# Input load on a second queue, the first norm ahead of the range chain, and one-hot operands widened by ScalarE

## The reference, cut to what matters

```
xn  = (x - mean(x)) / sqrt(var(x) + 1e-5)          # per node
hp  = xn @ W                                        # 625 x 512 by 512 x 512
agg = segment_sum(hp[src] * edge_w[:, None], dst)   # 20000 edges into 625 nodes
x   = x + relu(agg) + linear_attention(xn)          # and then everything else
```

## Time and profile before

| | us |
|---|---|
| median of 3 runs (lowest, highest) | 1215.78 (1212.98, 1218.05) |
| the profiled execution, its own time | 1213.48 |
| its span in the trace | 1211.9 |
| TensorE busy | 1091.0 (90%) |
| VectorE busy | 553.2 (46%) |
| ScalarE busy | 362.5 (30%) |
| GpSimd busy | 118.4 (10%) |
| window loop, first matmul | 42.49 after the span's start |

### The profile page before, as it was taken

One profiled execution on the slowest core, in us unless ns is written; L12 is line 12 of the kernel. 1 busy time (PEld: TensorE's weight loads), 2 busy tenths in 40 slices (PEclk: granted clock), 3 DMA queues, 4 the chain that ended last, 5 costly groups with the idle time before them and its releaser, 6 DMA issues.

```text
span 1211.9 us, 20096 instructions
## 1 busy us (share of the span) xinstructions
PE 1091.0 (90%) x7246; PEld 732.4 (60%) x7247; DVE 553.2 (46%) x1370; ACT 362.5 (30%) x919; POOL 118.4 (10%) x183
## 2 busy tenths in 40 slices
PE   4788999999998749999997399999999999987898
PEld 2577746467775515555553277787577778554653
DVE  7888748644544501111111335453405545865340
ACT  1012212045554301122222145553135455022330
POOL 1013360020000420111110230000000000000000
PEclk9999999999999669999999699999999999998899
DMA  4000384000000679400999350000111000000001
GB/s 125 35 1 2 100 211 200 0 27 27 28 1 1 244 249 396 185 17 17 371 412 389 92 233 27 28 27 6 65 53 44 27 10 2 35 1 0 1 9 34
DMA packets 19105, 113.09 MB, mean 93 GB/s; under 512 B 4906, under 2 KB 6433, under 8 KB 14948
## 3 DMA queue, kind: packets, MB, share of 16 engines
q1 hardware_dynamic: 13406, 100.95, 22.1%
q0 software_dynamic: 5632, 11.23, 3.5%
HBM read 103.04 MB, written 9.11 MB: 93 GB/s over the span
## 4 chain that ended last, share of the span: by engine, by line
PE 78%; DVE 10%; DMA 5%; issue 3%; ACT 2%; DVEq 1%; POOL 1%; SPq 0%; POOLq 0%; ACTq 0%
PE psum L768 9%; PE psum L588 8%; PE psum L936 8%; PE psum L917 7%; PE psum L791 6%; PE psum L822 5%; PE psum L773 5%; PE psum L804 5%; PE psum L655 4%; PE psum L1021 3%; PE psum L1043 3%; PE psum L606 3%; DMA arena<-in_moe_b 3%; PE psum L949 2%; PE psum L727 2%
## 5 line engine op out<-in xcount | busy, mean ns | idle before, releaser
L588 PE MATMUL psum<-arena 128*125 128x512 f32 x320 | 142.2, 600 | 0.0
L1138 ACT ACTIVATE arena<-arena,small 125x625 f32<-125x625 f32 x120 | 97.0, 809 | 89.9 <-DVE small L1499 89.9
L768 PE MATMUL psum<-arena 128*128 128x313 f32 (+1 forms) x384 | 110.6, 438 | 2.0 <-ACT arena L1077 0.7
L917 PE MATMUL psum<-arena 128*64 128x512 f32 x448 | 100.3, 601 | 6.4 <-DMA arena<-in_moeW 4.9
L1203 ACT ACTIVATE arena<-psum,cols 128x64 f32<-128x64 f32 x224 | 47.5, 361 | 194.4 <-PE psum L923 194.4
L588 PEld LDWEIGHTS psum<-arena 128*125 128x125 f32 x320 | 60.2, 191 | 72.7 <-issue 71.2
L936 PE MATMUL psum<-arena 128*64 128x256 f32 x896 | 99.8, 381 | 3.6 <-DMA arena<-in_moe_b 1.9
L768 PEld LDWEIGHTS psum<-arena 128*128 128x128 f32 x384 | 71.2, 192 | 30.7 <-issue 2.2
L1499 DVE CUSTOM_DVE_ANT_0 arena<-psum,cnt_adj 125x625 f32<-125x625 f32 x80 | 61.5, 806 | 59.1 <-PE psum L791 59.1
L1146 ACT ACTIVATE arena<-psum 125x500 f32<-125x500 f32 x120 | 63.8, 584 | 81.9 <-PE psum L804 81.9
L936 PEld LDWEIGHTS psum<-arena 128*64 128x64 f32 x896 | 63.4, 137 | 36.1 <-ACT arena L1203 5.2
(11 more groups left out here) (266 smaller groups left out, 1402.7 us busy)
## 6 DMA issues: line engine op xcount, KB each, us to landing
arena<-in_moeW SPq DMA_DIRECT2D x16, 4096.0 KB, 17.9
arena<-in_att SPq DMA_DIRECT2D x36, 256.0 KB, 2.8
arena<-in_l1W SPq DMA_DIRECT2D x2, 2048.0 KB, 15.9
token_rows<-arena POOLq DMA_DIRECT2D x19, 128.0 KB, 5.1
rows<-in_rows SPq DMA_DIRECT2D x1, 2240.0 KB
expert_rows<-arena POOLq DMA_DIRECT2D x17, 128.0 KB, 4.9
arena<-token_rows POOLq DMA_DIRECT2D x16, 128.0 KB, 7.8
arena<-in_gnnWo SPq DMA_DIRECT2D x2, 1024.0 KB, 6.2
```

What stands on the lines that cost most here:

```text
L588: mm = pe.matmul(bank(b, NP, D), srcT[:, k, c * NP:(c + 1) * NP], w[:, k, :], start=(k == 0), stop=(k == KC - 1))
L768: mm = pe.matmul(bank(b, P, width), aw[:, w, k, :], srcT[:, k, o:o + width], start=(k == 0), stop=(k == KC - 1))
L917: mm = pe.matmul(psum[q * TT:(q + 1) * TT, 512 * b:512 * b + D], xsT[:, k4, :], EW1[par][:, k4, o:o + D], start=(k4 == 0), stop=(k4 == KC ...
L1138: act.activation(Sx[u % 3][h], Sx[u % 3][h], ACT.Exp, bias=small[0:NP, 80 + n:81 + n], scale=-1.0, accum_out=small[0:NP, 120 + n:121 + n]) ...
```

## The change

Three things are done. The two loads of x are issued by ScalarE at its start and no longer by SP behind the edge loads; ScalarE also runs one dummy square root, which brings its table load forward. VectorE applies the first norm ahead of the range chain, and TensorE makes the sum over windows behind the first `hp` chunk and the bounds row behind the second, in banks 2 and 3. And the operands with an innermost step of 0 are written out by ScalarE (`widened`) into `hot_dst` itself, in two halves of 82 and 83 tiles, so that VectorE compares and multiplies in place, on rows of 32 packed 16-bit values; four passes of 5280 elements become eight of 2624 or 2656.

```
@@ block.sync
-            for p in SPLIT:
-                sp.dma_start(xres[p], ins["x"][p]).then_inc(ld_x, 16)
             sp.wait_ge(ld_x, 32)
@@ block.tensor
-            pe.wait_ge(range_cols, 1)
-            pe.matmul(bank(5, NW, WMIN), upper[0:NW, 0:NW], w_loops, start=True, stop=True).then_inc(range_cum, 1)
             rows_to_cols("xnT0", N1, lambda c: pe.wait_ge(ln_out, c + 1))
             stage_out(pe, "xnT0")
+            ring_ready(0)
+            product_chunk("hp", T1, ring[0], 0)
+            pe.wait_ge(range_cols, 1)
+            pe.matmul(bank(2, NW, WMIN), upper[0:NW, 0:NW], w_loops, start=True, stop=True).then_inc(range_cum, 1)
+            product_chunk("hp", T1, ring[0], 1)
             pe.wait_ge(range_cols, 2)
-            pe.matmul(bank(4, 1, WMIN), w_cols[:, 2:3], ident[0:NW, 0:WMIN],
+            pe.matmul(bank(3, 1, WMIN), w_cols[:, 2:3], ident[0:NW, 0:WMIN],
                       start=True, stop=True).then_inc(range_rows, 1)
-            product_rows("hp", T1, 0)
+            for c in range(2, NC):
+                product_chunk("hp", T1, ring[0], c)
...
-            pe.wait_ge(dst_one, 1)
-            pe.wait_ge(dst_parts, 3)
+            pe.wait_ge(dst_one, 2)
+            pe.wait_ge(dst_parts, 6)
@@ block.scalar
+            for p in SPLIT:
+                act.dma_start(xres[p], ins["x"][p]).then_inc(ld_x, 16)
+            act.wait_ge(consts, 2)
+            act.activation(small[0:1, 94:95], onesf[0:1, 0:1], ACT.Sqrt)
+
+            def widened(dst, src, t, ready):
+                n = t.stop - t.start
+                act.activation(dst[:, t, :], src[:, t].unsqueeze(2).to_broadcast([NP, n, DW]), ACT.Copy).then_inc(ready, 1)
+
+            act.wait_ge(edge_low, 1)
+            for t in tile_halves:
+                widened(hot_dst4[:, :, 3, :], low, t, wide_low)
+            act.wait_ge(edge_parts, 3)
+            widened(hot_dst4[:, :, 0, :], w_part[:, 0, :], tile_halves[0], wide_parts)
             deviation(0)
+            widened(hot_dst4[:, :, 0, :], w_part[:, 0, :], tile_halves[1], wide_parts)
             cols_out("xnT0", T1)
+            for v in (1, 2):
+                for t in tile_halves:
+                    widened(hot_dst4[:, :, v, :], w_part[:, v, :], t, wide_parts)
             rows_out("hp", N2)
@@ block.vector
             norm_moments()
+            norm_apply(0, xres, N1)
             ve.wait_ge(range_turned, 1)
...
-            norm_apply(0, xres, N1)
             ve.wait_ge(range_cum, 1)
...
-            ve.tensor_tensor(hot_dst4[:, :, 3, :], low.unsqueeze(2).to_broadcast([NP, TP, DW]),
-                             iota_dst.unsqueeze(1).to_broadcast([NP, TP, DW]), ALU.is_equal).then_inc(dst_one, 1)
             ve.wait_ge(range_rows, 1)
-            ve.tensor_copy(bounds, bank(4, 1, WMIN)).then_inc(range_ready, 1)
-            ve.wait_ge(dst_one, 1)
+            ve.tensor_copy(bounds, bank(3, 1, WMIN)).then_inc(range_ready, 1)
+            for h, t in enumerate(tile_halves):
+                ve.wait_ge(wide_low, h + 1)
+                ve.tensor_tensor(hot_dst4[:, t, 3, :], hot_dst4[:, t, 3, :],
+                                 iota_dst.unsqueeze(1).to_broadcast([NP, t.stop - t.start, DW]),
+                                 ALU.is_equal).then_inc(dst_one, 1)
+            ve.wait_ge(dst_one, 2)
             for v in range(3):
-                ve.tensor_tensor(hot_dst4[:, :, v, :], hot_dst4[:, :, 3, :],
-                                 w_part[:, v, :].unsqueeze(2).to_broadcast([NP, TP, DW]), ALU.mult).then_inc(dst_parts, 1)
+                for h, t in enumerate(tile_halves):
+                    ve.wait_ge(wide_parts, 2 * v + h + 1)
+                    ve.tensor_tensor(hot_dst4[:, t, v, :], hot_dst4[:, t, v, :], hot_dst4[:, t, 3, :],
+                                     ALU.mult).then_inc(dst_parts, 1)
```

More of the change, by code:

```diff
@@ L175, in build @@
         hot_dst = arena[0:NP, o_D:o_D + TP * 2 * DW].bitcast(BF16)
+        tile_halves = [slice(0, TP // 2), slice(TP // 2, TP)]
         hot_dst4 = hot_dst.rearrange("p (t v d) -> p t v d", v=4, d=DW)
@@ L289, in build @@
         dst_one, dst_parts = sem("dst_one"), sem("dst_parts")
+        edge_low, edge_parts, wide_low, wide_parts = (
+            sem("edge_low"), sem("edge_parts"), sem("wide_low"), sem("wide_parts"))
         hot_ready, hot_free = sem("hot_ready"), sem("hot_free")
@@ L1334, in _ @@
             ve.wait_ge(win_ready, 1)
-            ve.tensor_copy(low[:, 0:ET], low_i)
-            ve.tensor_copy(w_part[:, 0, 0:ET], w_hi)
+            ve.tensor_copy(low[:, 0:ET], low_i).then_inc(edge_low, 1)
+            ve.tensor_copy(w_part[:, 0, 0:ET], w_hi).then_inc(edge_parts, 1)
             ve.scalar_tensor_tensor(key[:, 0:ET], win, 1024.0, srcf, ALU.mult, ALU.add)
@@ L1339, in _ @@
             link(ve.tensor_scalar(w_mid.bitcast(I32), w_rest.bitcast(I32), -65536, None, ALU.bitwise_and))
-            ve.tensor_copy(w_part[:, 1, 0:ET], w_mid)
-            ve.tensor_tensor(w_part[:, 2, 0:ET], w_rest, w_mid, ALU.subtract)
+            ve.tensor_copy(w_part[:, 1, 0:ET], w_mid).then_inc(edge_parts, 1)
+            ve.tensor_tensor(w_part[:, 2, 0:ET], w_rest, w_mid, ALU.subtract).then_inc(edge_parts, 1)
             ve.wait_ge(consts, 16)
@@ L1369, in _ @@
             ve.tensor_copy(w_loops, n_i[:, 1:2].to_broadcast([NW, WMIN])).then_inc(range_cols, 1)
-            ve.scalar_tensor_tensor(w_cols[:, 1:2], w_cols[:, 0:1], 64.0, n_i[:, 1:2], ALU.mult,
-                                    ALU.add)
-            norm_apply(0, xres, N1)
+            link(ve.scalar_tensor_tensor(w_cols[:, 1:2], w_cols[:, 0:1], 64.0, n_i[:, 1:2], ALU.mult,
+                                         ALU.add))
             ve.wait_ge(range_cum, 1)
-            ve.scalar_tensor_tensor(w_cols[:, 2:3], bank(5, NW, 1), 16384.0, w_cols[:, 1:2], ALU.mult,
+            ve.scalar_tensor_tensor(w_cols[:, 2:3], bank(2, NW, 1), 16384.0, w_cols[:, 1:2], ALU.mult,
                                     ALU.add).then_inc(range_cols, 1)
-            ve.tensor_tensor(hot_dst4[:, :, 3, :], low.unsqueeze(2).to_broadcast([NP, TP, DW]),
-                             iota_dst.unsqueeze(1).to_broadcast([NP, TP, DW]), ALU.is_equal).then_inc(dst_one, 1)
             ve.wait_ge(range_rows, 1)
-            ve.tensor_copy(bounds, bank(4, 1, WMIN)).then_inc(range_ready, 1)
-            ve.wait_ge(dst_one, 1)
+            ve.tensor_copy(bounds, bank(3, 1, WMIN)).then_inc(range_ready, 1)
[5 more added lines that the diff above has]
+            ve.wait_ge(dst_one, 2)
             for v in range(3):
-                ve.tensor_tensor(hot_dst4[:, :, v, :], hot_dst4[:, :, 3, :],
-                                 w_part[:, v, :].unsqueeze(2).to_broadcast([NP, TP, DW]), ALU.mult).then_inc(dst_parts, 1)
+                for h, t in enumerate(tile_halves):
+                    ve.wait_ge(wide_parts, 2 * v + h + 1)
+                    ve.tensor_tensor(hot_dst4[:, t, v, :], hot_dst4[:, t, v, :], hot_dst4[:, t, 3, :],
+                                     ALU.mult).then_inc(dst_parts, 1)
             ve.wait_ge(range_ready, 1)
```

## The result

| | before | after |
|---|---|---|
| median of 20 runs (lowest, highest), us | 1215.67 (1212.02, 1218.83) | 1218.93 (1213.52, 1222.55) |
| span of the profiled execution, us | 1211.9 | 1219.8 |
| window loop, first matmul, us after the start | 42.49 | 47.18 |

The ratio is 1.0025, 95% interval 1.0014 to 1.0037: slower by 3 us, within the half per cent that counts as no change here. The time forecast was 1217.3, and the measured 1218.93 lies in the range given, 1211.5 to 1221.5.

A forecast was written before the change was run, and what follows sets the result against it. The start-up was taken as bound by VectorE, about 1 us ahead of TensorE, and by the edges' landing; reordering -2.1 and later edges +3.7 gave +1.6 us, 1215.1 profiled, 1217.3 as median with 2.30 added; range 1211.5 to 1221.5.

The forecast's parts named there:

- (b): Rival: VectorE's in-place passes do not run packed and stay at 5.64 us each; +10.9 and +1.6, 1228.2 us; chance 0.07.
- D: Moment the edge loads land and VectorE starts: 6.06 us before, forecast 9.8, later by 3.7, bounds 0 and 4.9 later.
- equal bytes: Edge loads and x share DMA engines with equal bytes from both queues; edges done at 8.1 us, landing at 8.8.
- x first: Upper bound for the edge loads: they land last on their DMA engines, behind x, at 11.0 us.
- From D to the loop: Start-up from the edges' landing to the window loop: D + 34.3 instead of D + 36.4, a gain of 2.1 us.
- VectorE's two waits ahead of `bounds`: VectorE was to stand idle for nearly 8 us while TensorE makes the sum and the row behind two `hp` chunks.
- The widening, not the statistics, set the root: On ScalarE, three widenings of 2.42 us end at D + 8.6, the variance at D + 8.0; root done at D + 8.8.
- Rival (a): The edge loads keep their time, D below 8.2, at best 6.06; -2.1 us at best, median 1213.7; chance 0.25.
- break-even at D = 8.2: Landing time of the edge loads at which the change neither gains nor loses: 8.2 us after the start.
- shortening VectorE's passes alone: Before the window loop VectorE leads TensorE's own way by about 1 us only, so this alone buys 1 us.
- Rival (c): VectorE's sequencer does not run six instructions ahead, so its register load ends at D + 37.8; +3.6 us, 1220.9; chance 0.10.
- The loop behind: The window loop, once started, takes the same time as before; otherwise the prediction is wrong altogether.

The follow-up runs named there:

- `a_again`: The changed kernel without an edit, run once more; median 1219.06 us, ratio 1.0037 to the kernel before.
- `a_x_on_sp`: The changed kernel with SP issuing x again, behind the three edge loads; median 1214.02 us, ratio 0.9991 to the kernel before.
- `h_widening_only`: The kernel before with ScalarE's widenings, the dummy root and the packed passes only; median 1214.59 us, ratio 0.9984 to the kernel before.
- `c_sum_first`: The changed kernel with x back on SP behind the edges, and TensorE's sum over windows ahead of the first `hp` chunk; 1211.76 us, ratio 0.9979 to before.
- `i_x_behind_table`: The changed kernel with x still issued by ScalarE, but only behind its table load and dummy root; 1215.72 us, ratio 0.9987 to the kernel before.

## Why the prediction was right, and where it was not

The forecast, slower by some 1.6 us and not measurably changed, held in sign and class. The class alone proves little, as all the rivals but (b) lay mostly within it, and the rise was about half of the 3.3 us between the two medians. Point by point:

- **D.** The term that was mis-sized. I took 9.8, between equal bytes (8.8) and x first (11.0). It was 11.25, 11.12 and 11.05 in three executions with x issued at 1.04, thus the upper bound. The model of equal bytes was wrong: from 4 us on the packet counts show about one edge row for one row of x, and a row of x is 16 times as large, so that only 105 of 375 edge rows are through at 8 us, and 121 of the 125 rows of x. That is 1.3 to 1.5 us more than was summed. The Trainium skill, DMA: Bandwidth & Descriptors, section Queues, rings and completion order, has the engines take turns packet by packet; had I priced it with one row of x for one edge row, as the counts from 4 us on have it, about 8 of the 75 edge rows of an engine would have passed beside its 8 rows of x, and D would have come out near the upper bound. The page's packets of some 9 to 17 descriptors are not what these counts show.
- **From D to the loop.** D + 34.3 was summed; `a_again` has 45.24 - 11.12 = 34.1. The parts: the root ends 8.4 behind D (summed 8.8), three widenings 6.97 (7.26), `hp` starts at D + 14.4 (14.7), halves 1.46 (1.45). VectorE's two waits ahead of `bounds`, summed as nearly 8 us, are 4.77 and 3.61 in `a_again`. The widening, not the statistics, set the root, as summed: it began at 19.46, when the third widening was through, 0.3 behind the variance. In `a_x_on_sp`, with x late, the statistics did.
- **The profiled run of after** starts its loop 1.9 later than `a_again`, at D + 35.9: the chunk at half rate, which the sum did not have.
- **Rival (a) and its 1213.7.** The edges did not keep their time, so (a) is out. Its sum was wrong besides: D + 34.3 took x as landed, and with D near 6 it is not, though the rows had x at 11.02 and the statistics ready for it at D + 4.19. `a_x_on_sp` has D at 6.17, a wait of 1.41, and the loop at D + 35.4: 0.9 us under the kernel before, 1.7 when both are counted from the landing of x, and not 2.1. By time it is 0.9991 (0.9972 to 1.0009), which shows no gain for certain. The break-even at D = 8.2 is untouched by this: there the statistics would start at 12.4, when x had landed in every run with that issue. Right was that shortening VectorE's passes alone buys little: `h_widening_only` buys 0.3 by the loop, 0.9984 by time.
- **Rival (b)**, unpacked passes, is out: 1.46 a half, 2.83 without the widening. Section 5.1 of the Vector Engine (DVE) Microarchitecture Reference of the Trainium skill gives such operands two elements a cycle, and the trace agrees: 11.7 us against 11.0, the estimate from its 0.96 GHz without a fixed cost.
- **Rival (c)** is out. The register load on VectorE's sequencer starts at 38.3, behind the compare, with six multiplies still ahead of it in the engine:

```profile
L342 DVEq TENSOR_LOAD <-arena x1: 1608/1608/1608, 38.3 to 38.3; - x1
```

- **The loop behind.** I had said that it would have to take the same time. From the loop's start to the end of the span it takes 1169.4 us before, 1172.6 after and 1172.7 in `a_again`, but from 1167.4 (`c_sum_first`) to 1175.6 (`i_x_behind_table`) in kernels that differ nowhere in it. The span of one execution therefore says little of a change of 3 us; the start of the loop and the medians say it.

## What to carry to other kernels

A load that is moved to another queue to start sooner also starts ahead of what the first queue has still to issue. Look which load the first consumer waits for, how large its rows are beside the mover's, and keep the large rows behind the small ones in time, on whichever queue. And when a long pass is shortened, ask by how much it led: here 10 us taken off VectorE's passes bought under 1 by the start of the loop (`h_widening_only`), and more came only with an earlier start of TensorE's work (`c_sum_first`, 2.4 by the loop, 0.9979 by time). Whether an earlier x adds to that the times do not tell.

## What the runs showed of the hardware that was not expected

**Small rows behind large ones.** Edge rows of 640 B, issued in the same 1.1 us as rows of 10 KB on a second queue, let VectorE start at 11.05 to 11.25 instead of 6.06; with x issued at 2.56, and its first rows moving before 4 us, it started at 5.62. Why the last hundred edge rows pass x there, and not in the first case, no run shows: turns of one row each would have held them up as well. It stays open.

**A chunk at half rate, and a granted clock of 1.00 that is not a record.** In the changed kernel's profile the weight loads of the first `hp` chunk come 0.85 us apart, then 0.43:

```profile
27.48 0.33 PEld L589 LDWEIGHTS psum<-arena 128*125 128x125 f32 x1 [0.52 <-issue]
...
30.09 0.19 PEld L589 LDWEIGHTS psum<-arena 128*125 128x125 f32 x1 [0.24 <-issue]
```

The granted clock of that stretch (third number from the end) reads full:

```profile
27.00:28.00 1.00, 1.00 (x2) 0.33 (x1) 0.00 (x0) 1.00 (x2) 0.00 (x0) 1.00 0.00 0
```

The column also reads 1.00 where the trace holds no record of the clock. The first record of this trace, at full clock, begins at 29.27 us, just where the weight loads change their pace. Five of the twelve profiles have such a stretch in `hp`, 1.6 to 2.0 us longer than without it, and in each of them the first record begins within that chunk, at the change of pace (29.27, 30.94, 27.64, 25.53, 24.23). In the other seven, the kernel before among them, it begins before `hp` does, between 19.79 and 24.93. So the slow part fits the lower of the two levels, 1.2 GHz, up to that record and 2.4 GHz from it on; no record shows the lower level itself. TensorE had turned the norm chunks from 20.51 on, after 4.6 idle us. `a_again` did the same work after the same idle time, and its first record begins 0.55 us ahead of `hp`: what decides between the two, no run shows.
